# A sandwich layer on one core: new orders for the mixing stage's queues, one burst of scores per group, and gating moved to VectorE

## The chip, the cores and the metric

The kernel runs on one NeuronCore of a Trainium2 chip. The metric is the device time of one execution in microseconds. TensorE is written PE, VectorE DVE, ScalarE ACT, GpSimd POOL; SP is the engine that only issues transfers.

## The reference

All data is float32. x is (8, 512, 256): 8 batch rows of 512 time steps.

```python
x = x + layernorm(attn(layernorm(x)))
x = x + layernorm(ffn(layernorm(x)))
# attn: gate, value_raw, params = x @ W_in.T;  value = silu(causal_conv4(value_raw))
# dt = clip(softplus(params0 + dt_bias));  kd = 0.5 * sigmoid(params1);  A = exp(A_log)
# bc = l2norm over 32 states of (value @ W_bc.T): Bz, Bx, Cz, Cx, for each of 32 heads
def step(carry, inp):          # 512 steps, state (32 heads, 32 states, 16 channels)
    S = 1.0 / (1.0 + dt * kd + dt * dt * A)
    z = S * (z - dt * A * s + dt * Bz * u)
    s = s + dt * z + dt * Bx * u
    y = sum_n(Cz * z) + sum_n(Cx * s)
# out = ((y + skip * value) * silu(gate)) @ W_out.T
# ffn: gelu(x @ ternary(W1).T + b1) @ ternary(W2).T + b2
```

## The kernel before, in words

`build` calls three stages, one after the other, each with its own block of five instruction queues: `project` (L83), `mix` (L423) and `ffn` (L1246). They hand their results over in DRAM scratch tensors. A `Signal` (L51) is a semaphore whose target for row b and item i is computed by `at`. It is credited: negative items are taken as already given.

**project** normalises x, multiplies by W_in, convolves, and writes value, gate, skip x value x gate, u and the step factors. The change leaves it alone.

**mix** turns the recurrence into chunks of 64 steps (8 chunks in a row). The 32 heads form 8 groups of 4 heads (4 x 32 states = 128 partitions); a batch row is done in two halves of 4 groups, here called phases: 16 phases in all, and `over_rows` loops over the batch rows, the last one written apart. In a phase, for its groups first to first + 3 and for the groups of the next half, `then` to then + 3:
- PE makes the next half's B and C by units (`product`, L689; 4 units per group, 4 matmuls of 128x512 over the contraction index kt per unit, into two PSUM banks used in turn), 5 units more than a half ahead. After a group's first unit it makes the previous group's sums of squares (`sum_squares`, L685). Between units it transposes keys (`transposes`, L714), multiplies them with u (`state_terms`, L726), makes the masked scores' products (`scores_and_unit`, L744: two pairs of heads, each 32 matmuls of 32x64, recorded as 64, each pair followed by half a unit), and the outputs (`outputs`, L766: 64 small matmuls with `g` and 28 with the block states `Xb`).
- ACT squares and copies each unit out of PSUM, starts the next load of weights, takes the root of the sums (`norms`, L822), copies transposed keys to `kT` (L857), states to `X` and `Xb`, and results to `y`.
- SP takes the norms of a group through a compact layout (`compact_norms`, L561), stores the finished scales to DRAM and loads them back spread over partitions, first the two for B (`input_scales`, L590), then, into the same buffer, the two for C (`output_scales`, L599). Every step is a wait followed by issues, in the order in L611 to L634. `load_valT` (L574) refills the moving operand of all units once per row, after unit 31 is done.
- POOL issues the loads of `shear` and `det`.
- DVE does, in the order written out in `phase` (L1194 to L1237): `scales` (L1024, on 128x64: waits for `compact`, counts `rows_ready`), `scale_inputs` (L1037, waits for SP's load, counts `b_scaled`), `scale_outputs` (L1045, the same, `c_scaled`), `keys` (L1069), `queries` (L1087), `det_sums`, `coefficients` (L1130), `states` (L1147, a chain over 7 chunks) and `mask` (L1120: ps_g x causal into `g`, once the outputs of the previous group have read it). Between all of these, `advance` interleaves the next phase's 128 psi steps (L1016, L1020) in proportion to a cost in ns that each operation gives; `advance(OF_PHASE)` issues those that are left.

`scores_and_unit` waits for `q_ready(group)` and for `g_ready(group - 1)`, as the score banks are single. `outputs` waits for `g_ready(group)`.

**ffn** works row by row. POOL gates y (`y * gate + svg`, L1387 and L1389, 128x2048 each). PE projects (`project_out`), ACT copies, DVE adds the normalised result to x (`first_residual`), normalises again (`second_norm`), PE transposes. The first product is taken in 8 tiles f with x split into a high and a low part (L1436), ACT applies Gelu (L1494) and copies the high part (L1496), DVE subtracts for the low part (L1598), PE makes the second product in four tiles t (L1449, 64 matmuls), DVE adds the bias (L1609), takes statistics of all four tiles, ACT takes the root (L1508), DVE normalises `o2` in place (L1531), adds x1 (L1621), ACT stores. Rows 0, 1, 6 and 7 are written out; 2 to 5 are a hardware loop of two rows. At the start SP loads y, gates, then both weights, which DVE makes ternary with three passes each (L1579 to L1582).

The order of PE's work in the second part of a phase, which the change touches:

```python
scores_and_unit(b, first, unit, last)
products(b, unit + 1, 1, last)
unit += 2
for i in range(1, HALF):
    scores_and_unit(b, first + i, unit, last)
    outputs(b, first + i - 1)
    products(b, unit + 1, 1, last)
    unit += 2
outputs(b, first + HALF - 1)
```

## Time and profile before

| what | us |
|---|---|
| median of 3 runs (2637.96 to 2643.87) | 2638.85 |
| the profiled execution | 2637.77 |
| its span | 2636.1 |
| PE busy | 2092.6 (79%) |
| DVE busy | 1921.2 (73%) |
| ACT busy | 956.8 (36%) |
| POOL busy | 385.6 (15%) |

The span runs from the first to the last instruction of one profiled execution; a busy time is the union of an engine's instructions. An engine's idle time before an instruction is put down to what released it last. PE's clock has two levels here, 1.0 (2.4 GHz) and 0.5 (1.2 GHz); a window's clock is the mean of what was granted. The stages are, by the span's time, `project` to about 294 us, `mix` to 2308 and `ffn` to the end.

### The profile page before, as it was taken

The page shows a single profiled execution, that of the slowest core. Times are in us where ns is not written, and L with a number is a line of the kernel's source. Part 1 is how long each engine was busy: PE and PEld are TensorE (multiplying, and loading weights), DVE is VectorE, ACT ScalarE, POOL GpSimd, SP SyncE. Part 2 cuts the span into 40 slices and gives each one's busy share as a digit, 9 for nine tenths or more (in the row PEclk, how much of TensorE's full clock was granted, in tenths as well). Part 3 has the DMA queues.
Part 4 walks back from the last instruction along what each step waited for, and adds up shares of the span by engine and source line. Part 5 has one row for each costly group of instructions (what it writes and reads, how often), then busy time and mean ns, then how long its engine had stood idle before and what let it go on. Part 6 is the DMA issues. An engine that isn't in the chain of part 4 may idle for free. (4 is left out here: it accounts for less than half of the span.)

```text
span 2636.1 us, 66597 instructions
## 1 busy us (share of the span) xinstructions
PE 2092.6 (79%) x25890; PEld 1258.7 (48%) x25890; DVE 1921.2 (73%) x4396; ACT 956.8 (36%) x1905; POOL 385.6 (15%) x604
## 2 busy tenths in 40 slices
PE   5777485887888988888878789998988887728886
PEld 2333132454454545444544445454544446626675
...
GB/s 96 172 171 163 148 127 82 134 100 131 96 137 99 131 103 136 109 111 131 104 129 97 135 95 130 115 135 111 107 134 101 137 83 85 14 253 127 127 25 24
DMA packets 240466, 306.05 MB, mean 116 GB/s; under 512 B 124960, under 2 KB 141344, under 8 KB 231968
## 3 DMA queue, kind: packets, MB, share of 16 engines
...
q10 hardware_dynamic: 85056, 94.40, 12.8%
...
## 5 line engine op out<-in xcount | busy, mean ns | idle before, releaser
L700 PE MATMUL m_ps_a<-m_valT,m_w_bc 128*128 128x512 f32 x2048 | 1037.3, 651 | 59.5 <-DMA m_valT<-scratch_valT 49.2
L700 PEld LDWEIGHTS m_ps_a<-m_valT,m_w_bc 128*128 128x128 f32 x2048 | 397.3, 206 | 472.9 <-issue 443.7
L651 POOL DMA_DIRECT2D m_shear<-scratch_shear x512 | 274.3, 537 | 1564.8 <-DVE m_psi L1020 1452.8
L835 ACT ACTIVATE m_sq<-m_ps_a 128x512 f32<-128x512 f32 x256 | 153.1, 598 | 651.7 <-PE m_ps_a L700 651.7
L759 PE MATMUL m_ps_g<-m_raw 32*64 32x64 f32 x8192 | 185.9, 249 | 166.9 <-DVE m_g L1124 141.3
L1020 DVE TENSOR_TENSOR m_psi<-m_psi,m_prod 128x128 f32<-128x128 f32 x1024 | 294.0, 287 | 19.6
L1016 DVE TENSOR_TENSOR m_prod<-m_psi,m_shear 128x128 f32<-128x128 f32 x1024 | 293.0, 286 | 18.0
L759 PEld LDWEIGHTS m_ps_g<-m_raw 32*64 32x64 f32 x8192 | 165.0, 159 | 268.4 <-issue 265.9
L1042 DVE TENSOR_TENSOR m_raw<-m_raw,m_scale 128x1024 f32<-128x1024 f32 x64 | 78.4, 1224 | 239.0 <-DMA m_scale<-scratch_norm 230.3
L784 PE MATMUL m_ps_k<-m_raw,m_Xb 128*112 128x64 f32 x1024 | 177.1, 306 | 0.0
L1079 DVE TENSOR_TENSOR m_part<-m_raw,m_psi 128x1024 f32<-128x1024 f32 x128 | 155.6, 1218 | 13.7 <-issue 13.2
L224 PE MATMUL ps_w<-p_xnT,w_in 128*128 128x512 f32 x256 | 130.5, 663 | 41.1 <-ACT vraw L282 36.0
L1110 DVE TENSOR_TENSOR m_part<-m_raw,m_psi 128x1024 f32<-128x1024 f32 x128 | 155.6, 1218 | 0.1
L784 PEld LDWEIGHTS m_ps_k<-m_raw,m_Xb 128*112 128x112 f32 x1024 | 150.9, 216 | 8.5 <-issue 3.7
L837 ACT ACTIVATE m_raw<-m_ps_a 128x512 f32<-128x512 f32 x256 | 152.5, 596 | 0.0
L897 ACT ACTIVATE m_y<-m_ps_y 112x256 f32<-112x256 f32 x64 | 24.6, 384 | 305.1 <-PE m_ps_k L784 305.1
L1124 DVE TENSOR_TENSOR m_g<-m_ps_g,m_causal 128x1024 f32<-128x1024 f32 x64 | 78.0, 1219 | 74.4 <-PE m_ps_k L784 74.3
L784 PE MATMUL m_ps_y<-m_raw,m_Xb 128*112 128x64 f32 x768 | 130.4, 303 | 0.0
L877 ACT ACTIVATE m_Xb<-m_X 32x224 f32<-32x224 f32 x256 | 98.7, 386 | 74.9 <-DVE m_X L1165 71.8
L1050 DVE TENSOR_TENSOR m_raw<-m_raw,m_scale 128x1024 f32<-128x1024 f32 x64 | 78.1, 1220 | 60.5 <-DMA m_scale<-scratch_norm 60.5
L784 PEld LDWEIGHTS m_ps_y<-m_raw,m_Xb 128*112 128x112 f32 x768 | 114.1, 218 | 0.0
L224 PEld LDWEIGHTS ps_w<-p_xnT,w_in 128*128 128x128 f32 x256 | 52.2, 212 | 115.8 <-issue 66.0
...
## 6 DMA issues: line engine op xcount, KB each, us to landing
m_scale<-scratch_norm SPq DMA_DIRECT2D x512, 128.0 KB
...
m_shear<-scratch_shear POOLq DMA_DIRECT2D x512, 64.0 KB, 2.9
...
```

The source lines that it names most:

```text
L224: mm = pe.matmul(ps_w[i % BANKS].ap(), w_in[:, k, col:col + P], xnT[:, k, :], start=(k == 0), stop=(k == KD - 1))
L651: pool.dma_start(shear[h * N:(h + 1) * N, w % 2].rearrange("p k g t -> p k (g t)"), spread(src)).then_inc(into.sem, into.step)
L700: mm = pe.matmul(ps_a[j % 2].ap(), w_bc[:, j, kt, :], valT[:, kt, :], start=(kt == 0), stop=(kt == KI - 1))
L759: mm = pe.matmul(ps_g[odd * C:(odd + 1) * C, at:at + C], raw[heads, group, p_, cols], raw[heads, group, NJ - 1 - p_, cols], start=(p_ == 0 ...
L784: mm = pe.matmul(ps_y[c % 2][0:ROWS, c // 2 * C:(c // 2 + 1) * C], Xb[:, c - 1, p_, :], raw[:, group, NJ - 1 - p_, c * C:(c + 1) * C], sta ...
L835: act.activation(sq[:, j, :], ps_a[j % 2].ap(), ACT.Square).then_inc(sq_ready.sem, sq_ready.step)
L837: act.activation(raw[:, group % HG, j, :], ps_a[j % 2].ap(), ACT.Copy).then_inc(raw_ready.sem, raw_ready.step)
L877: ins = act.activation(Xb[heads, :, :, h * N:h * N + DH], X[heads, 0:NC - 1, :, group % HALF, :], ACT.Copy)
L1016: dve.tensor_tensor(prod.ap().rearrange("p k g r -> p (k g) r"), psi_kt[of_half][:, :, t, :], window.unsqueeze(2).to_broadcast([P, 2 * HAL ...
L1020: ins = dve.tensor_tensor(psi_t[of_half][:, :, :, t + 1, :], psi_t[of_half][:, :, :, t, :], prod[:, ::-1, :, :], ALU.add)
L1079: dve.tensor_tensor(in_pairs(part[:, k]), pairs(raw[:, slot, k, :]), psi[:, half % 2, k, g_, :, at:at + C, :], ALU.mult).then_inc(own.sem, ...
L1110: dve.tensor_tensor(in_pairs(part[:, k]), pairs(raw[:, group, 3 - k, :]), psi[:, half, k, g_, :, 1:, :], ALU.mult).then_inc(own.sem, own.o ...
```

## The change

In `mix`: SP and DVE issue the steps of the scales in a new order; the masked scores go in turn to `g` and to `kT`, so that a mask waits for the outputs of two groups back; the first mask of a phase is issued in the middle of `states`; each quarter of valT is loaded when unit 31's matmul on it is done; `scores_and_unit` becomes `scores` (both pairs, 64 matmuls recorded as 128) followed by whole units. In `ffn`: gating moves from POOL to DVE, three rows ahead; the second product, its bias and statistics go in two halves with the transposes between them; PE's projection goes in two parts; the normalisation and residual of a row are issued at the start of the next; all rows are written out; both weights are loaded from ACT's queue, and are made ternary in two passes each.

```diff
@@ -477,6 +477,7 @@
+        masked = [g.ap(), kT.ap().rearrange("p a (b h c) -> p a b h c", b=2, h=HP)]
@@ -503,6 +504,7 @@
+        val_used = sig("val_used", KI - 1)
@@ -573,6 +575,8 @@
 
     def load_valT(b):
         for kt in range(KI):
+            if not (isinstance(b, int) and b == 0):
+                sp.wait_ge(val_used.sem, val_used.at(b - 1, kt)) if kt < KI - 1 else sp.wait_ge(a_made.sem, a_made.at(b - 1, UNITS - 1))
             sp.dma_start(valT[:, kt, :], dram["valT"][b, :, kt, :]).then_inc(val_in[kt].sem, val_in[kt].step)
 
     def load_e_end(b, half):
@@ -622,14 +626,12 @@
                 input_scales(b, then + 1)
                 output_scales(b, then + 1)
                 norm_rows(b, then + 2)
+                input_scales(b, then + 2)
             if half == 0 and not last:
-                sp.wait_ge(a_made.sem, a_made.at(b, UNITS - 1))
                 load_valT(b + 1)
             if more:
-                input_scales(b, then + 2)
                 output_scales(b, then + 2)
                 norm_rows(b, then + 3)
-            if more:
                 input_scales(b, then + 3)
                 output_scales(b, then + 3)
     over_rows(sp, body)
@@ -699,6 +701,8 @@
+            if unit == UNITS - 1 and kt < KI - 1:
+                mm.then_inc(val_used.sem, val_used.step)
@@ -741,7 +745,7 @@
-    def scores_and_unit(b, group, unit, last):
+    def scores(b, group):
@@ -761,7 +765,6 @@
-            product(b, unit, last, pair * 2, pair * 2 + 2)
@@ -776,7 +779,7 @@
-                              u[rows, s, tile, h * DH:(h + 1) * DH], g[rows, h % 2, h // 2, tile, :],
+                              u[rows, s, tile, h * DH:(h + 1) * DH], masked[s % 2][rows, h % 2, h // 2, tile, :],
@@ -798,11 +801,12 @@
                 products(b, unit + 1, 1, last)
                 state_terms(b, first + i)
                 unit += 2
-            scores_and_unit(b, first, unit, last)
-            products(b, unit + 1, 1, last)
+            scores(b, first)
+            products(b, unit, 2, last)
             unit += 2
             for i in range(1, HALF):
-                scores_and_unit(b, first + i, unit, last)
+                scores(b, first + i)
+                products(b, unit, 1, last)
                 outputs(b, first + i - 1)
                 products(b, unit + 1, 1, last)
                 unit += 2
@@ -1120,8 +1124,8 @@
-        dve.wait_ge(y_made.sem, y_made.at(b, group - 1))
-        dve.tensor_tensor(g.ap().rearrange("p a h c t -> p (a h c) t"),
+        dve.wait_ge(y_made.sem, y_made.at(b, group - 2))
+        dve.tensor_tensor(masked[group % 2].rearrange("p a h c t -> p (a h c) t"),
@@ -1144,7 +1148,7 @@
-    def states(b, half, advance):
+    def states(b, half, advance, between):
@@ -1165,6 +1169,8 @@
+            if c == NC // 2 - 1:
+                between()
@@ -1206,35 +1212,33 @@
         det_sums(b, half, advance)
         if more:
             scale_outputs(b, then, advance)
+            scales(b, then + 1, advance)
         keys(b, first + 3, advance)
         queries(b, first, advance)
+        if more:
+            scale_inputs(b, then + 1, advance)
         queries(b, first + 1, advance)
         if more:
-            scales(b, then + 1, advance)
+            scale_outputs(b, then + 1, advance)
+            scales(b, then + 2, advance)
         coefficients(b, half, advance)
-        states(b, half, advance)
-        mask(b, first, advance)
+        states(b, half, advance, lambda: mask(b, first, advance))
         if more:
-            scale_inputs(b, then + 1, advance)
+            scale_inputs(b, then + 2, advance)
         queries(b, first + 2, advance)
         mask(b, first + 1, advance)
         if more:
-            scale_outputs(b, then + 1, advance)
-            scales(b, then + 2, advance)
+            scale_outputs(b, then + 2, advance)
+            scales(b, then + 3, advance)
         queries(b, first + 3, advance)
-        if more:
-            scale_inputs(b, then + 2, advance)
         mask(b, first + 2, advance)
         if more:
-            scale_outputs(b, then + 2, advance)
-            scales(b, then + 3, advance)
+            scale_inputs(b, then + 3, advance)
         advance(OF_PHASE)
-        if more:
-            scale_inputs(b, then + 3, advance)
         mask(b, first + 3, advance)
         if more:
+            scale_outputs(b, then + 3, advance)
             keys(b, then, stepping(b, half + 2, not last))
-            scale_outputs(b, then + 3, advance)
 
     def body(b, last):
         for half in range(2):
@@ -1322,22 +1326,16 @@
-        o2_made = sig("o2_made", 1)
+        o2_made = sig("o2_made", 2)
@@ -1380,14 @@
-@block.gpsimd
-def _(pool):
-    pool.sem_inc(gated.sem, gated.given * gated.step)
...
-        pool.tensor_tensor(y[s].ap(), y[s].ap(), gate[s].ap(), ALU.mult).then_inc(own.sem, own.one())
-        pool.wait_ge(own.sem, own.n)
-        pool.tensor_tensor(y[s].ap(), y[s].ap(), svg[s].ap(), ALU.add).then_inc(gated.sem, gated.step)
...
-    rows(pool, body)
@@ +1418,32 @@
+    def second(b, half_):
+        for t in range(2 * half_, 2 * half_ + 2):
+            for f in range(KF):
+                for part in (gh, gl):
+                    mm = pe.matmul(ps_2[half_][:, t % 2, :], part[:, f, t * P:(t + 1) * P], t2[:, f, :],
...
+        mm.then_inc(o2_made.sem, o2_made.step)
+
+    def body(b, s, left):
+        pe.wait_ge(xl_ready.sem, xl_ready.at(b, KD - 1))
+        for f in range(2):
+            hidden(b, f)
+        if left > 1:
+            for t in range(2):
+                project_out(b + 2, s, t)
+        for f in range(2, KF):
+            hidden(b, f)
+        if left > 1:
+            for t in range(2, TT):
+                project_out(b + 2, s, t)
+        pe.wait_ge(gl_ready.sem, gl_ready.at(b, KF - 1))
+        pe.wait_ge(o2_ready.sem, o2_ready.at(b, -1))
+        second(b, 0)
+        if left:
+            transpose_xn(b + 1)
+        second(b, 1)
@@ +1449,2 @@
+    for n, (dst, name) in enumerate(((w1, "w1T"), (w2, "w2T"))):
+        act.dma_start(dst.ap(), a[name].rearrange("(k p) o -> p k o", p=P)).then_inc(weight_in[n], 16)
@@ -1536,7 +1530,14 @@
-    def first_residual(b, s, i):
+    def gating(b):
+        s = b % 2
+        dve.wait_ge(y_in[s].sem, y_in[s].at(b // 2, y_in[s].per - 1))
+        dve.tensor_tensor(y[s].ap(), y[s].ap(), gate[s].ap(), ALU.mult).then_inc(own.sem, own.one())
+        dve.wait_ge(own.sem, own.n)
+        dve.tensor_tensor(y[s].ap(), y[s].ap(), svg[s].ap(), ALU.add).then_inc(gated.sem, gated.step)
+
+    def first_residual(b, s):
@@ +1566,30 @@
+    def second_bias(b, half_):
+        dve.wait_ge(o2_made.sem, o2_made.at(b, half_))
+        rows_ = range(2 * half_, 2 * half_ + 2)
+        ins = dve.tensor_tensor(o2[:, 2 * half_:2 * half_ + 2, :], ps_2[half_].ap(),
+                                b2.ap().unsqueeze(1).to_broadcast([P, 2, D]), ALU.add)
+        if half_:
+            ins.then_inc(o2_ready.sem, o2_ready.step)
+            dve.wait_ge(o2_ready.sem, o2_ready.at(b, 0))
+        else:
+            ins.then_inc(own.sem, own.one())
+            dve.wait_ge(own.sem, own.n)
+        for t in rows_:
+            dve.bn_stats(stats2[:, t, :], o2[:, t, :]).then_inc(own.sem, own.one())
+        dve.wait_ge(own.sem, own.n)
+        for t in rows_:
+            ins = dve.bn_aggr(mv[2][:, t, :], stats2[:, t, :])
+            ins.then_inc(own.sem, own.one()) if t < TT - 1 else ins.then_inc(var2_ready.sem, var2_ready.step)
+    def second_residual(b):
+        dve.wait_ge(sd2_ready.sem, sd2_ready.at(b, 0))
+        dve.reciprocal(rstd[2].ap(), sd[2].ap()).then_inc(own.sem, own.one())
+        dve.wait_ge(own.sem, own.n)
+        normalise(on, lambda t: o2[:, t, :], 2)
+        dve.wait_ge(own.sem, own.n)
+        dve.wait_ge(res_stored.sem, res_stored.at(b, -1))
+        dve.tensor_tensor(res.ap(), x1[b % 2].ap(), on.ap(), ALU.add).then_inc(res_ready.sem, res_ready.step)
+        dve.wait_ge(res_ready.sem, res_ready.at(b, 0))
@@ -1579,20 @@
-        dve.tensor_scalar(above.ap(), w, half[:, n:n + 1], None, ALU.is_gt).then_inc(own.sem, own.one())
-        dve.tensor_tensor(tern.ap().rearrange("p k o -> p (k o)"), above.ap(), below.ap(),
-                          ALU.subtract).then_inc(ternary_ready, 1)
+        dve.scalar_tensor_tensor(out=tern.ap().rearrange("p k o -> p (k o)"), in0=w, scalar=half[:, n:n + 1],
+                                 in1=below.ap(), op0=ALU.is_gt, op1=ALU.subtract).then_inc(ternary_ready, 1)
+        if n == 0:
+            gating(1)
@@ +1627,25 @@
+    def body(b, s, left):
+        if b:
+            second_residual(b - 1)
         for f in range(KF):
             dve.wait_ge(gh_ready.sem, gh_ready.at(b, f))
             dve.tensor_tensor(gl[:, f, :], g[:, f, :], gh[:, f, :].bitcast(F32), ALU.subtract).then_inc(gl_ready.sem, gl_ready.step)
             if left and f == KF // 2 - 1:
-                first_residual(b + 1, 1 - s, i + s)
+                first_residual(b + 1, 1 - s)
         if left:
             second_norm(b + 1, 1 - s)
         if left > 1:
             projection_moments(b + 2)
+        second_bias(b, 0)
         if left:
             low_part(b + 1)
-        dve.wait_ge(o2_made.sem, o2_made.at(b, 0))
-        for half_ in range(2):
-            ins = dve.tensor_tensor(o2[:, 2 * half_:2 * half_ + 2, :], ps_2[half_].ap(),
-                                    b2.ap().unsqueeze(1).to_broadcast([P, 2, D]), ALU.add)
-            ins.then_inc(o2_ready.sem, o2_ready.step) if half_ else ins.then_inc(own.sem, own.one())
-        moments(lambda t: o2[:, t, :], 2, var2_ready)
...
-        normalise(o2, lambda t: o2[:, t, :], 2)
...
+        if left > 2:
+            gating(b + 3)
+        second_bias(b, 1)
...
```

## Rows read from the trace of the kernel before

**Rows 1.** Windows: stretch, length, PE PEld DVE ACT POOL busy (count), clock, DMA.
```profile
473.80:2159.60 1685.80, 1454.40 (x21282) 838.67 (x21281) 1326.41 (x3095) 611.86 (x1302) 267.15 (x502) 0.89 0.44 117
2159.60:2308.00 148.40, 103.94 (x2137) 89.81 (x2135) 95.00 (x181) 35.40 (x86) 8.32 (x16) 0.56 0.20 53
2308.00:2374.00 66.00, 19.11 (x75) 15.64 (x75) 38.39 (x50) 5.32 (x10) 27.01 (x6) 0.66 0.79 254
2374.00:2636.10 262.10, 202.68 (x1016) 171.04 (x1016) 176.16 (x387) 120.43 (x191) 45.90 (x10) 0.86 0.22 75
```

**Rows 2.** L1135, first instruction of `coefficients`: count, ns min/median/max, first and last start.
```profile
L1135 DVE TENSOR_TENSOR m_end<-m_det,m_e_end x16: 190/194/197, 473.8 to 2251.3; 128x28 f32<-128x28 f32 x16
```

**Rows 3.** Groups by line, DVE: busy us, mean ns | idle before, releasers.
```profile
L1042 DVE TENSOR_TENSOR m_raw<-m_raw,m_scale 128x1024 f32<-128x1024 f32 x64 | 78.4, 1224 | 239.0 <-DMA m_scale<-scratch_norm 230.3 <-ACT m_raw L837 6.9 <-issue 1.8
...
L1050 DVE TENSOR_TENSOR m_raw<-m_raw,m_scale 128x1024 f32<-128x1024 f32 x64 | 78.1, 1220 | 60.5 <-DMA m_scale<-scratch_norm 60.5
...
L1124 DVE TENSOR_TENSOR m_g<-m_ps_g,m_causal 128x1024 f32<-128x1024 f32 x64 | 78.0, 1219 | 74.4 <-PE m_ps_k L784 74.3
...
L1027 DVE TENSOR_SCALAR m_compact<-m_compact 128x64 f32<-128x64 f32 x64 | 12.1, 189 | 37.3 <-DMA m_compact<-m_rows 37.3
```

**Rows 4.** Groups by line, PE, same columns.
```profile
L759 PE MATMUL m_ps_g<-m_raw 32*64 32x64 f32 x8192 | 185.9, 249 | 166.9 <-DVE m_g L1124 141.3 <-issue 24.3 <-DVE m_raw L1116 0.3
...
L778 PE MATMUL m_ps_y<-m_g,m_u 64*16 64x64 f32 x2048 | 47.8, 241 | 68.8 <-DVE m_g L1124 68.8
...
L700 PE MATMUL m_ps_a<-m_valT,m_w_bc 128*128 128x512 f32 x2048 | 1037.3, 651 | 59.5 <-DMA m_valT<-scratch_valT 49.2 <-issue 7.4 <-ACT m_raw L837 2.8
```

**Rows 5.** Timeline of DVE in one phase: start us, us, line [idle before].
```profile
1760.73 0.23 DVE L1034 TENSOR_TENSOR m_compact<-m_compact,m_factor 128x64 f32<-128x64 f32 x1
...
1768.87 1.23 DVE L1042 TENSOR_TENSOR m_raw<-m_raw,m_scale 128x1024 f32<-128x1024 f32 x1 [2.55 <-DMA m_scale<-scratch_norm]
...
1830.36 0.22 DVE L1034 TENSOR_TENSOR m_compact<-m_compact,m_factor 128x64 f32<-128x64 f32 x1
...
1843.38 1.23 DVE L1042 TENSOR_TENSOR m_raw<-m_raw,m_scale 128x1024 f32<-128x1024 f32 x1 [5.01 <-DMA m_scale<-scratch_norm]
...
1849.87 1.22 DVE L1050 TENSOR_TENSOR m_raw<-m_raw,m_scale 128x1024 f32<-128x1024 f32 x1 [2.75 <-DMA m_scale<-scratch_norm]
...
1853.06 0.20 DVE L1027 TENSOR_SCALAR m_compact<-m_compact 128x64 f32<-128x64 f32 x1 [1.43 <-DMA m_compact<-m_rows]
```

**Rows 6.** The same timeline: `queries(first)` and `queries(first + 1)` begin.
```profile
1785.74 1.22 DVE L1093 TENSOR_TENSOR m_raw<-m_raw,m_det 128x1024 f32<-128x1024 f32 x1
...
1793.32 1.22 DVE L1093 TENSOR_TENSOR m_raw<-m_raw,m_det 128x1024 f32<-128x1024 f32 x1
```

**Rows 7.** Timeline of PE: start us, us, line; same phase, then the last phase.
```profile
1812.90 1.98 PE L759 MATMUL m_ps_g<-m_raw 32*64 32x64 f32 x64 [6.97 <-DVE m_g L1124]
...
1829.13 1.07 PE L685 MATMUL m_ps_s<-m_sq,m_head_sum 128*32 128x512 f32 x8
...
2260.84 4.04 PE L759 MATMUL m_ps_g<-m_raw 32*64 32x64 f32 x128 [6.10 <-DVE m_g L1124]
```

**Rows 8.** Windows of that phase's second half and of the last phase, columns of rows 1.
```profile
1812.90:1819.30 6.40, 6.40 (x96) 3.75 (x100) 5.94 (x14) 0.34 (x1) 2.14 (x4) 0.50 0.51 128
...
2187.90:2308.00 120.10, 85.28 (x1843) 78.47 (x1835) 72.55 (x115) 27.78 (x69) 3.82 (x8) 0.50 0.19 50
```

**Rows 9.** Groups by line, feed-forward stage, columns of rows 3; last: of rows 2.
```profile
L1531 DVE TENSOR_SCALAR f_o<-f_o,f_mv,f_rstd 128x256 f32<-128x256 f32 x32 | 33.7, 1115 | 0.3
...
L1609 DVE TENSOR_TENSOR f_o<-f_ps,f_b 128x512 f32<-128x512 f32 x16 | 10.3, 686 | 52.3 <-PE f_ps L1449 52.3
...
L1389 POOL TENSOR_TENSOR f_y<-f_y,f_svg 128x2048 f32<-128x2048 f32 x8 | 36.7, 4590 | 0.6
...
L1531 DVE TENSOR_SCALAR f_o<-f_o,f_mv,f_rstd x32: 400/408/4735, 2410.2 to 2631.0; 128x256 f32<-128x256 f32 x32
```

**Rows 10.** L1621, last DVE instruction of a row: columns of rows 2.
```profile
L1621 DVE TENSOR_TENSOR f_res<-f_x,f_o x8: 1224/1224/1227, 2416.7 to 2631.5; 128x1024 f32<-128x1024 f32 x8
```

108 lines of the change are left out of this document (38 added, 70 removed).

## The prediction

> **What bounds the kernel now.** The profiled execution took 2637.77 us (span 2636.1 and 1.7 around it), 1.1 below the median of the three runs, 2638.85; all sums below start from 2637.8. I read the page first (PE 79% busy, DVE 73%: no engine is full), then windows by stage, the idle time by line, and the timeline of single phases. The mixing stage is 1.7 ms of 2.6: 14 equal phases fill 1685.8 us, 120.4 each, with DVE busy 94.7 and PE 103.9 in each [rows 1, 2]. At the mean clock of 0.89 some 26 us of a phase run at 1.2 GHz, so PE's work at 2.4 GHz would be about 104 - 13 = 91 us. Neither engine can be the bound alone at 120: they wait for each other and for DMA, in a ring.
>
> The waits are these. DVE stands for the normalising scales, which go by SP out to DRAM and back, 230.3 and 60.5 us; before the mask, 74.3, until the outputs of the previous group have left `g`; for `compact`, 37.3 [rows 3]. PE stands for the masked scores, 141.3 and 68.8 us [rows 4]. One trip of the scales takes from `rows_ready` to the scaled input 7.9 us in the one case and 12.8 in the other [rows 5]. The input of `then + 2` and `then + 3` have little DVE work in that time, so DVE waits; PE, behind it, waits too, falls to 1.2 GHz and works more slowly when it resumes, as at 1812.90 after 6.97 us of idleness [rows 7, 8].
>
> **The change, mixing stage.** (1) DVE's order: each `scales` is issued one place earlier, so that more vector work covers a trip. A 128x1024 operation with its share of psi steps costs 1.9 us (`queries`, 7.6 us [rows 6], is four such by size). After the change the cover is: input `then`, one `keys`, 5.7, unchanged; `then + 1`, `keys` and `queries`, 13.3; `then + 2`, coefficients, states and one mask, about 11.5; `then + 3`, `queries` and a mask, 9.5. Against trips of 7.9 to 12.8 [rows 5] that leaves waits of 3.0, 0.5, 0.5 and 1.0. Output scales follow `b_scaled` by 5.3 us or so (input begins 1843.38 and lasts 1.2, output begins 1849.87 [rows 5]): all have 7.6 or more of cover, except `then + 3`, which now stands ahead of `keys(then)` and has a mask and the last five steps, 2.7 us. I put 3.8 there, a new wait (bounds 0 and 6).
>
> (2) `scales(then + 3)` now stands before `queries(first + 3)`. It needs the sum of squares that PE makes after unit 32. From the first scores after `mask(first)` to the end of that sum PE took 1812.90 to 1830.20, 17.3 us [rows 7], and the burst changes the order within it, not the work. The square root, four issues on SP and the landing I estimate at 4.9 (the whole tail of input scale, output issues and compact took 8.5, 1844.6 to 1853.06 [rows 5], and is the upper bound). DVE has in that time three of seven state steps (3.8 by the code's own costs), input scale, `queries`, mask and output scale, together 17.1. So 5 us of waiting stand there that did not before (bounds 0 and 9).
>
> (3) The second masked buffer lets `mask(g)` wait for `y_made(g - 2)`: the 74.3 us go [rows 3], a part of them in the last phase. That `g_made` is not the next wait rests on the `queries` between; were PE a whole `outputs` late, 1 to 2 us a mask would stay. `mask(first)` in mid-states lets PE resume 4 us earlier, and is the start of the chain in (2). PE's two mask waits per group become one long one, about 9 us at the second group, since PE needs 91 of the period.
>
> (4) The burst: a group's two score halves follow each other, then a whole unit. The last phase has the same form already: 128 recorded matmuls took 4.04 us at half clock, against 1.98 for 64 [rows 7]; no price, within 0.1 us a group. If PE's queue can't fetch so many small ones at 2.4 GHz, up to 1 us a group, in PE's slack.
>
> (5) valT by quarters, loads released by `val_used`: part of 49.2 us of PE waits [rows 4]; the one at the stage's start stays. On SP it is now behind `input_scales(then + 2)` but ahead of the output scales, which wait with it for unit 31 in every first half: 3 to 4 us late, inside the 9.5 of cover. Priced 0, bounds -5 and +10 us in all.
>
> DVE is idle 25.7 us in each of the 14 phases [rows 1]. The four waits are 402.4 us, 25.2 for each of 16 phases [rows 3]; a part of that lies before the first phase and in the last, and some 2 us of the 25.7 are gaps between instructions, so I take 23.5 for a middle phase. After: 5.0 for input scales, 3.8, 5.0, and nothing for masks: 13.8, less 0.3 where one delay hides another. That is 10 us a phase, a period near 110.5. The sum: 14 x 10 = 140, 8 in the interval after, and 6 in the last phase.
>
> By the Trainium skill ("DMA: Bandwidth & Descriptors", Latency and other measured facts) a transfer has a fixed cost of about 2 us, so two hops would be some 4 and the input waits would vanish. Rows 5 say 7.9 and more; with the page's figure the period would be about 105.
>
> **The change, feed-forward stage.** A row takes (2631.5 - 2416.7) / 7 = 30.7 us, and over the whole stretch 262.1 / 8 = 32.8 [rows 1, 10]. Removed: GpSimd's two products (4.59 and about the same again [rows 9]), and with them the stall of DVE's normalisation of `o`, 1115 ns mean where the median is 408 [rows 9], (1115 - 408) x 4 = 2.8 us a row, and by an estimate half as much, 1.5, at the other two normalisations. Added: the same two on DVE, four 128x1024 pieces at 1.22 [rows 3], 4.9 us a row. DVE waits 52.3 / 8 = 6.5 a row for the second product [rows 9]; gating now lies in that gap, and the product is split so that its bias and statistics start half way and only half of them (1.6 us) precede the next row's Gelu; the normalisation and residual of the row move into the next row's Gelu time, 3 us. Sum: 4.9 - 4.3 added, 1.6 + 3 taken from the chain, and about 1 for the projection in two parts: 5 a row, 40 in all over 8 rows. One pass fewer on the weights and their load on ACT's queue move the start by 0 to 5 us; the first row still waits for the same bytes at 254 GB/s [rows 1]. Priced 0. Bounds of the stage: -3 (gating fully exposed) and 60 (all of DVE's 6.5 too).
>
> The forecast: 2637.8 - 140 - 8 - 6 - 40 = 2444, say 2445 us.
>
> **Rivals.** A, waits change place: the new chain of (2) costs its 9, the output wait 6, feed-forward gives 25. For it: SP is one queue, and each trip is issued behind a wait. Phase gain 5: 2637.8 - 70 - 8 - 6 - 25 = 2529. B, trips shorten once less collides, and nearly no DVE wait remains: period 105, which is DVE's 94.7 busy [rows 1], 2 of gaps and 8 for the two trips without cover, 2637.8 - 14 x 15.4 - 14 - 45 = 2363. Against: DMA gets denser with a shorter period. C, slower: PE stays at 1.2 GHz. The one long idle stretch ahead of a burst of 32-row matmuls is where the clock falls; the last phase, all burst and outputs, ran at 0.50 for 120 us while PE was 71% busy [rows 8]. With x us of a phase's full-clock work at half clock the period is 91 + x and a few us; beyond x = 32, 123.3, the loss exceeds the feed-forward's gain. With x = 40, period 133: 2637.8 + 176 - 40 = 2774. Against: in 1812.90 to 1819.30 the clock came back after 6.4 us with the same bursts between units [rows 8], and 512-wide units follow here as there.
>
> By the Trainium skill ("TensorE: Matmul & The Clock Gate", Part 4) transposes do not count as PE activity, which speaks for C in each phase's first half; rows 1's 0.89 for the same mixture does not bear it out. D: the order helps but gating on DVE makes that engine the feed-forward's bound, gain 0 there: 2484. That burst and order change nothing at all is excluded by the instructions moved.
>
> **Chances and range.** Forecast and its neighbourhood (2395 to 2490, D within it) 0.62, A 0.18, B 0.13, C 0.04, and 0.03 for gains and losses that cancel. The range goes from 2380 to 2535, leaving out C, the farther half of B and the edge of A. A measurement of this kernel tells about 0.2%, 5 us. Faster 0.94, same 0.01, slower 0.05.
>
> **What would show it.** L1135's starts 110 us apart (right), 116 or more (A), 106 or less (B). L1042's wait for scales under 6 us a phase, L1124's gone, L1027's near 5, L1050's near 4. One PE wait a phase of 8 to 10 us at L759; granted clock over the phases 0.89 or above; below 0.8 is C. Feed-forward rows 28 us apart, no wait at the bias above 3. Wrong would be: a DVE wait that none of these names, or PE idle for less than 3 us a phase.

## The result and the profile after

The changed kernel took 2480.61 us (median of 4 runs, 2478.51 to 2491.96) beside 2638.55 for the kernel before on the same chip: a ratio of 0.9406 [0.9375, 0.9437], 158 us less. The forecast was 2445 and the range 2380 to 2535: faster as said, inside the range and 35.6 us above the likeliest value. The profiled execution took 2482.11 us, its span 2480.4. On another chip the same kernel gave 2482.13, ratio 0.9414 [0.9389, 0.9439]. The kernel before has medians of 2630.6 to 2638.9 on the chips used, so what is compared below is ratios.

The windows by stage, in the columns and for the stages of [rows 1]. The bounds moved with the stages: the first to the fifteenth start of `coefficients`, then to the end of `mix`, then the feed-forward's start, then its rows.

```profile
482.40:2062.30 1579.90, 1426.94 (x21285) 823.59 (x21283) 1322.34 (x3095) 612.50 (x1303) 267.26 (x504) 0.91 0.46 125
2062.30:2190.10 127.80, 97.72 (x2128) 86.77 (x2128) 90.00 (x170) 34.25 (x84) 6.20 (x12) 0.57 0.19 51
2190.10:2235.00 44.90, 9.36 (x34) 7.70 (x34) 15.90 (x13) 2.37 (x3) 0.00 (x0) 0.61 0.94 262
2235.00:2480.40 245.40, 200.28 (x1056) 160.07 (x1056) 193.99 (x439) 121.30 (x198) 0.00 (x0) 0.95 0.28 101
```

The 14 middle phases take 1579.9 us where they took 1685.8: 112.85 each, against 120.4 before and 110.5 forecast. DVE is busy 94.5 us in each, as before; what went is its idle time. The first line of `coefficients` [rows 2] and the feed-forward's residual [rows 10], by source line, give the rest:

```profile
L1139 DVE TENSOR_TENSOR m_end<-m_det,m_e_end x16: 193/196/200, 482.4 to 2138.9; 128x28 f32<-128x28 f32 x16
```
```profile
L1591 DVE TENSOR_TENSOR f_res<-f_x,f_on x8: 1224/1225/1226, 2289.6 to 2475.9; 128x1024 f32<-128x1024 f32 x8
```

`mix` ends (the feed-forward's first DVE instruction) at 2190.1 where it ended at 2309.3: 119.2 us less, where 154 were forecast. That is 105.9 in the 14 phases, 15.0 in the interval after (91.6 to 76.6), 6.8 in the tail, less 8.6 by which the first start came later. The feed-forward stage takes 290.3 us instead of 326.8: 36.5 less, where 40 were forecast. Its rows end 27.8 us apart at first and 26.6 in the mean, against 30.7 before and 28 forecast. Nearly the whole miss is in the mixing stage's phases.

The groups by line over the whole execution, DVE's and PE's, answer to [rows 3, 4]:

```profile
L1046 DVE TENSOR_TENSOR m_raw<-m_raw,m_scale 128x1024 f32<-128x1024 f32 x64 | 78.2, 1223 | 111.9 <-DMA m_scale<-scratch_norm 111.9
L1054 DVE TENSOR_TENSOR m_raw<-m_raw,m_scale 128x1024 f32<-128x1024 f32 x64 | 78.2, 1221 | 65.8 <-DMA m_scale<-scratch_norm 65.8
...
L1128 DVE TENSOR_TENSOR m_g<-m_ps_g,m_causal 128x1024 f32<-128x1024 f32 x32 | 39.0, 1219 | 1.0 <-PE m_ps_g L763 1.0
L1128 DVE TENSOR_TENSOR m_kT<-m_ps_g,m_causal 128x1024 f32<-128x1024 f32 x32 | 39.0, 1218 | 9.6 <-PE m_ps_g L763 9.6
...
L1031 DVE TENSOR_SCALAR m_compact<-m_compact 128x64 f32<-128x64 f32 x64 | 12.2, 191 | 93.0 <-DMA m_compact<-m_rows 93.0
```
```profile
L702 PE MATMUL m_ps_a<-m_valT,m_w_bc 128*128 128x512 f32 x2048 | 1029.1, 651 | 68.5 <-DMA m_valT<-scratch_valT 45.4 <-issue 17.4 <-ACT m_raw L841 5.7
...
L763 PE MATMUL m_ps_g<-m_raw 32*64 32x64 f32 x8192 | 200.3, 261 | 140.5 <-DVE m_g L1128 110.6 <-issue 22.7 <-DVE m_raw L1120 1.8
```

The input scales' wait has halved, the masks' has fallen from 74.4 to 10.6 (all of it behind the middle phases), `compact`'s has grown by 56, the output scales' by 5. PE's second mask wait (68.8 at the outputs) is gone. This is the pattern the forecast drew. Its sizes need the same view cut to the 14 middle phases, which the prediction didn't take. Before (473.8 to 2159.6):

```profile
L1042 DVE TENSOR_TENSOR m_raw<-m_raw,m_scale 128x1024 f32<-128x1024 f32 x56 | 68.6, 1224 | 206.4 <-DMA m_scale<-scratch_norm 197.7 <-ACT m_raw L837 6.9 <-issue 1.8
L1050 DVE TENSOR_TENSOR m_raw<-m_raw,m_scale 128x1024 f32<-128x1024 f32 x56 | 68.3, 1219 | 41.6 <-DMA m_scale<-scratch_norm 41.6
L1124 DVE TENSOR_TENSOR m_g<-m_ps_g,m_causal 128x1024 f32<-128x1024 f32 x56 | 68.2, 1219 | 45.7 <-PE m_ps_k L784 45.6
...
L1027 DVE TENSOR_SCALAR m_compact<-m_compact 128x64 f32<-128x64 f32 x56 | 10.6, 189 | 13.2 <-DMA m_compact<-m_rows 13.2
```

and after (482.4 to 2062.3):

```profile
L1083 DVE TENSOR_TENSOR m_part<-m_raw,m_psi 128x1024 f32<-128x1024 f32 x112 | 136.7, 1220 | 21.7 <-issue 21.3 <-DVE m_prod L1020 0.4
...
L1046 DVE TENSOR_TENSOR m_raw<-m_raw,m_scale 128x1024 f32<-128x1024 f32 x56 | 68.5, 1222 | 82.7 <-DMA m_scale<-scratch_norm 82.7
L1054 DVE TENSOR_TENSOR m_raw<-m_raw,m_scale 128x1024 f32<-128x1024 f32 x56 | 68.4, 1221 | 45.6 <-DMA m_scale<-scratch_norm 45.6
...
L1031 DVE TENSOR_SCALAR m_compact<-m_compact 128x64 f32<-128x64 f32 x56 | 10.7, 191 | 69.5 <-DMA m_compact<-m_rows 69.5
```

A middle phase had (206.4 + 41.6 + 45.7 + 13.2) / 14 = 21.9 us of named waits, not 23.5, and has (82.7 + 45.6 + 69.5) / 14 = 14.1, not 13.5. (Of the 206.4 the scales' DMA ended 197.7; with that part alone the 21.9 would be 21.3.) The 21.7 before L1083 is a gap inside `keys` of about 3 us once a row, where the loop over the rows turns: 1.5 a phase, 0.9 before (13.2 over 14 phases). By place, the timeline has the input scales waiting 3.2 us at `then`, nothing at `then + 1` and `then + 2`, and 2.7 at `then + 3`.

### The profile page after: what moved, and what is told of

Its sections match the earlier page's. It is cut to its first block and busy times, and to the rows that moved or that the text cites. A ratio compares the mean times of both kernels' runs of the same rounds, so it can differ in the third digit from the quotient of the medians.

```text
span 2480.4 us, 66343 instructions
## 1 busy us (share of the span) xinstructions
PE 2055.9 (83%) x25890; PEld 1226.2 (49%) x25890; DVE 1912.4 (77%) x4410; ACT 955.2 (39%) x1905; POOL 311.4 (13%) x588
## 5 line engine op out<-in xcount | busy, mean ns | idle before, releaser
L702 PEld LDWEIGHTS m_ps_a<-m_valT,m_w_bc 128*128 128x128 f32 x2048 | 407.8, 209 | 524.4 <-issue 502.8
L763 PE MATMUL m_ps_g<-m_raw 32*64 32x64 f32 x8192 | 200.3, 261 | 140.5 <-DVE m_g L1128 110.6
L1020 DVE TENSOR_TENSOR m_prod<-m_psi,m_shear 128x128 f32<-128x128 f32 x1024 | 292.4, 286 | 15.7
L763 PEld LDWEIGHTS m_ps_g<-m_raw 32*64 32x64 f32 x8192 | 178.0, 170 | 189.1 <-issue 172.5
L1083 DVE TENSOR_TENSOR m_part<-m_raw,m_psi 128x1024 f32<-128x1024 f32 x128 | 155.8, 1220 | 22.3 <-issue 21.3
L787 PE MATMUL m_ps_k<-m_raw,m_Xb 128*112 128x64 f32 x1024 | 156.4, 279 | 0.1
L787 PEld LDWEIGHTS m_ps_k<-m_raw,m_Xb 128*112 128x112 f32 x1024 | 131.1, 191 | 7.4 <-issue 0.8
L787 PE MATMUL m_ps_y<-m_raw,m_Xb 128*112 128x64 f32 x768 | 115.0, 276 | 0.0
L1387 PE MATMUL f_ps_o<-f_w_out,f_y 128*128 128x256 f32 x256 | 63.9, 407 | 48.0 <-DVE f_y L1538 48.0
L742 PEld LDWEIGHTS m_ps_k<-m_u,m_kT 64*32 64x32 f32 x7168 | 69.1, 109 | 62.6 <-issue 62.4
L787 PEld LDWEIGHTS m_ps_y<-m_raw,m_Xb 128*112 128x112 f32 x768 | 98.7, 191 | 0.0
```

The source lines that it names most:

```text
L702: mm = pe.matmul(ps_a[j % 2].ap(), w_bc[:, j, kt, :], valT[:, kt, :], start=(kt == 0), stop=(kt == KI - 1))
L763: mm = pe.matmul(ps_g[odd * C:(odd + 1) * C, at:at + C], raw[heads, group, p_, cols], raw[heads, group, NJ - 1 - p_, cols], start=(p_ == 0 ...
L787: mm = pe.matmul(ps_y[c % 2][0:ROWS, c // 2 * C:(c // 2 + 1) * C], Xb[:, c - 1, p_, :], raw[:, group, NJ - 1 - p_, c * C:(c + 1) * C], sta ...
L1020: dve.tensor_tensor(prod.ap().rearrange("p k g r -> p (k g) r"), psi_kt[of_half][:, :, t, :], window.unsqueeze(2).to_broadcast([P, 2 * HAL ...
L1083: dve.tensor_tensor(in_pairs(part[:, k]), pairs(raw[:, slot, k, :]), psi[:, half % 2, k, g_, :, at:at + C, :], ALU.mult).then_inc(own.sem, ...
```

## The chain inside one phase

The timeline of PE, DVE and SP's queue in one phase shows step (2) of the forecast at work (lines between left out):

```profile
1502.73 4.04 PE L763 MATMUL m_ps_g<-m_raw 32*64 32x64 f32 x128 [5.02 <-DVE m_g L1128]
...
1519.32 1.06 PE L687 MATMUL m_ps_s<-m_sq,m_head_sum 128*32 128x512 f32 x8
1520.31 2.41 PE L763 MATMUL m_ps_g<-m_raw 32*64 32x64 f32 x128
```
```profile
1501.37 1.22 DVE L1128 TENSOR_TENSOR m_g<-m_ps_g,m_causal 128x1024 f32<-128x1024 f32 x1
...
1525.27 0.20 DVE L1031 TENSOR_SCALAR m_compact<-m_compact 128x64 f32<-128x64 f32 x1 [5.22 <-DMA m_compact<-m_rows]
...
1541.25 1.22 DVE L1046 TENSOR_TENSOR m_raw<-m_raw,m_scale 128x1024 f32<-128x1024 f32 x1 [5.29 <-DMA m_scale<-scratch_norm]
```
```profile
1521.15 2.74 SPq L567 DMA_DIRECT2D m_compact<-m_rows  x4
1526.41 0.35 SPq L597 DMA_DIRECT2D scratch_norm<-m_compact  x1
1532.40 11.81 SPq L574 DMA_DIRECT2D m_scale<-scratch_norm  x8
```

The first mask releases PE, whose burst begins at 1502.73; the sum of squares ends at 1520.38, 17.65 us later (forecast 17.3); `compact` is there at 1525.27, 4.9 later (forecast 4.9); DVE has waited 5.22 (forecast 5). Then the trip to DRAM: the store is issued at 1526.41, and the loads wait for it until 1532.40, 6 us for the first hop alone. The scaled input starts at 1541.25, 14.8 us after the store was issued. The trips were taken as 7.9 to 12.8 [rows 5].

This phase is the second half of a row. In the seven second halves DVE waits 5.2 us in the mean for `compact` of `then + 3`. In the seven first halves it waits 2.6 there, since it has stood 3.7 for the output scales of `then + 2` just before. The rest of `compact`'s 69.5 us lies at other groups, 1.1 a phase.

## Experiments

Every kernel below computes the whole result. Ratios are against the kernel before on the same chip; a "period" is the distance of the first and fifteenth start of `coefficients`, divided by 14, in the profiled execution. It comes from that one execution: the changed kernel has 112.85, and 112.70 on the other chip.

**The two stages apart.** `mix_only` has `mix` as changed and `ffn` as before, `ffn_only` the reverse. Each is the diff above up to this line of `ffn`, or from it on:

```diff
-        o2_made = sig("o2_made", 1)
+        o2_made = sig("o2_made", 2)
```

> The new mixing stage with the feed-forward stage of before. In the two traces the mixing stage ends 119.2 us earlier and the feed-forward stage is 36.5 us shorter. If the two stages are independent: 2638.6 - 119 = 2519 us, and the phases stay 112.8 us apart. If a part of the gain of one stage comes from the other (caches of instructions, state left by the stage ahead), the sum of this run's gain and the next one's differs from 158 by more than 5 us.

> The mixing stage of before with the new feed-forward stage. Independent stages: 2638.6 - 37 = 2602 us.

Measured: 0.9542 [0.9495, 0.9588], period 112.59, and 0.9848 [0.9799, 0.9896], feed-forward stage 292.4 us. The two gains add to 0.0610, the whole change's is 0.0594. The difference is well inside the intervals, which would hide an effect of one stage on the other up to some 18 us; the period and the stage's length in the two traces, 0.3 and 2.1 us from the changed kernel's, show none. Three quarters of the gain is the mixing stage's.

**One masked buffer again.**

```diff
-        masked = [g.ap(), kT.ap().rearrange("p a (b h c) -> p a b h c", b=2, h=HP)]
+        masked = [g.ap(), g.ap()]
...
-                    dve.wait_ge(y_made.sem, y_made.at(b, group - 2))
+                    dve.wait_ge(y_made.sem, y_made.at(b, group - 1))
```

> After, but all masked scores go to g, so that a mask waits for the outputs of the group before, as in before. The forecast gave the second buffer the 74.3 us of mask waits. If it is worth that now: the mask of groups 1 to 3 waits for y_made 3 to 5 us a phase, 50 to 75 us slower, 2530 to 2555. If the order of DVE alone had removed them (more vector work between two masks): 0 to 15 us slower.

Measured: 0.9562 [0.9523, 0.9601], period 115.36. The mask's wait in the 14 middle phases is back, and part of the others has gone:

```profile
L1046 DVE TENSOR_TENSOR m_raw<-m_raw,m_scale 128x1024 f32<-128x1024 f32 x56 | 68.4, 1221 | 82.9 <-DMA m_scale<-scratch_norm 82.9
L1128 DVE TENSOR_TENSOR m_g<-m_ps_g,m_causal 128x1024 f32<-128x1024 f32 x56 | 68.3, 1219 | 66.3 <-PE m_ps_k L787 65.9
...
L1054 DVE TENSOR_TENSOR m_raw<-m_raw,m_scale 128x1024 f32<-128x1024 f32 x56 | 68.2, 1218 | 27.6 <-DMA m_scale<-scratch_norm 27.5
...
L1031 DVE TENSOR_SCALAR m_compact<-m_compact 128x64 f32<-128x64 f32 x56 | 10.6, 189 | 56.5 <-DMA m_compact<-m_rows 56.5
```

A wait of 66 us costs 2.5 x 14 = 35 in the phases: the other half is taken from the output scales (45.6 to 27.6) and from `compact` (69.5 to 56.5), which had been waiting while DVE now stands elsewhere. By its ratio the kernel is some 40 us slower than the changed one, between the two expectations: the order of DVE had not removed the wait, but the buffer is worth less than its wait.

**The first mask behind `states` again.**

```diff
-                    states(b, half, advance, lambda: mask(b, first, advance))
+                    states(b, half, advance, lambda: None)
+                    mask(b, first, advance)
```

> After, with the first mask behind the states again. By the chain that I gave (mask, scores, unit 31, outputs, unit 32, sum of squares, compact) everything from there on comes 3.8 us later while DVE's work up to scales(then + 3) is the same in sum, so the wait at compact grows by 3.8 us a phase, less what the outputs had waited for Xb: 30 to 55 us slower, 2511 to 2536. Rival (the chain is bound at Xb, which the states make, not at the mask): within 10 us of after.

Measured: 0.9654 [0.9616, 0.9692], period 117.3, 4.45 more than the changed kernel; by its ratio some 65 us slower, more than either theory had said. `compact` waits 100.6 us in the 14 phases (7.2 a phase for 5.0) and the scales 159.6 (11.4 for 9.2); PE's clock over them is 0.90, and PE's own wait for a mask at the scores 150.8 us for 97.8. Of the pieces of the mixing stage that were taken back it is the largest. PE is released later by the states' second half, and the chain to the last scales starts that much later. In second halves this falls on `compact` of `then + 3` (9.1 us for 5.2), in first halves on the output scales of `then + 2` (7.3 for 3.7), which stand behind unit 31.

**The scores' two pairs apart again**, each ahead of half a unit, all else as changed.

```diff
-                def scores(b, group):
+                def scores_and_unit(b, group, unit, last):
...
+                        product(b, unit, last, pair * 2, pair * 2 + 2)
```

> After, with the score pairs apart again and half a unit behind each, all else as after. My theory (the burst has no price, what misses from the 140 us was a size of the waits): 2481 within 5 us. Rival (the burst holds PE up by 2 us or more a phase, in fetch or clock, and that is a part of the 34 us that the phases fell short): faster by 14 us or more, under 2467. A gain from the burst itself: over 2486.

Measured: 0.9370 [0.9334, 0.9406], period 111.58, clock over the phases 0.93 against 0.91. PE's group of the scores in the middle phases, after and with the pairs apart:

```profile
L763 PE MATMUL m_ps_g<-m_raw 32*64 32x64 f32 x7168 | 170.2, 256 | 124.2 <-DVE m_g L1128 97.8 <-issue 20.1 <-DVE m_raw L1120 1.8
```
```profile
L763 PE MATMUL m_ps_g<-m_raw 32*64 32x64 f32 x7168 | 152.7, 239 | 130.4 <-DVE m_g L1128 109.4 <-issue 16.6 <-DVE m_raw L1120 4.1
```

The burst makes the scores dearer by (170.2 - 152.7) / 14 = 1.25 us a phase, and PE more busy by 1.7, at a slightly lower clock. Step (4) gave it no price. The intervals of the two kernels overlap, so over the whole kernel it may cost nothing, and the ratio's equivalent of 2472 us lies between this run's two theories (2481 within 5, under 2467). A gain from the burst, which would have been a ratio above the changed kernel's, isn't seen: this part of the change is not where its time comes from.

**Three edits against the waits that are left**, each by itself. `valt_later` puts valT's loads behind the output scales of `then + 2`; `outputs_after_keys` puts the output scales of `then + 3` behind `keys(then)` again; `sums_early` makes the second unit, and so the sums of squares, ahead of the first group's outputs (ACT's `norms` moves with it).

```diff
+                            output_scales(b, then + 2)
                         if half == 0 and not last:
                             load_valT(b + 1)
                         if more:
-                            output_scales(b, then + 2)
```
```diff
-                        scale_outputs(b, then + 3, advance)
                         keys(b, then, stepping(b, half + 2, not last))
+                        scale_outputs(b, then + 3, advance)
```
```diff
                             scores(b, first + i)
-                            products(b, unit, 1, last)
+                            products(b, unit, 2 if i == 1 else 1, last)
                             outputs(b, first + i - 1)
-                            products(b, unit + 1, 1, last)
+                            if i > 1:
+                                products(b, unit + 1, 1, last)
```

> After, with SP's load_valT behind output_scales(then + 2) in place of ahead of it. In every first half of a row DVE waits 3.7 us for these scales; I had priced that at 0. If the wait comes from SP standing in load_valT for unit 31, it goes from 3.7 to under 0.5, 7 times; but the sum of squares behind it (compact, 2.3 to 5 us) is next, and takes most of it: 0 to 15 us faster, 2466 to 2481. If valT now lands later than unit 32 wants it: PE's wait for valT grows from 1.1 us and the run is no faster. If the wait is the DMA queues' own and not SP's order, 3.7 stays.

> After, with scale_outputs(then + 3) behind keys(then), as before. It loses the wait of 1.2 to 2.5 us that I had forecast as new at 3.8. But the next compact is then released no earlier, since SP issues it after the output load, which waits for nothing of DVE but b_scaled. 1.5 us a phase if nothing takes it: 20 us faster, 2461. If the wait passes on to the next trip (scale_inputs(then), which waits 3 to 4 us after scales): within 5 us of after.

> After, with unit 32 and the sum of squares behind it ahead of outputs(first), and ACT's root of it ahead of its copy of y. The sum comes 3.7 us earlier. If the new wait at compact is bound by this chain, it goes from 4.2 us a phase to under 1 and the period from 112.8 to 109.5: 2481 - 45 = 2436. Rival (another trip takes its place: the scales of then + 3, or in first halves the output scales behind load_valT, or valT itself, which unit 32 now wants 3.7 us sooner): under 20 us faster.

Measured: 0.9391 [0.9354, 0.9427], 0.9372 [0.9334, 0.9410] and 0.9360 [0.9313, 0.9406]; periods 111.88, 112.08 and 111.91. Waits a phase, from the groups of the middle phases: scales 9.2 after, then 6.5, 6.6 and 9.0; `compact` 5.0, then 6.6, 7.3 and 3.8. The first two edits remove their wait, and each time the next one grows: the scales' 2.6 us less of `valt_later` give 0.97 of period (in first halves the wait for `compact` of `then + 3` goes from 2.6 to 6.0), the 2.5 of `outputs_after_keys` give 0.77. `sums_early` is another case: `compact` loses 1.2 and the scales hardly change. In second halves it does what it should: the chain from the first burst to the sum takes 14.3 us instead of 17.6 in the mean, and the wait for `compact` of `then + 3` falls from 5.2 to 1.9. In first halves the chain takes 17.9 for 18.8 and that wait is 3.3 for 2.6, since unit 32, wanted sooner, now waits for valT, the rival that the expectation named. PE's group of the units in the middle phases, after and in `sums_early`:

```profile
L702 PE MATMUL m_ps_a<-m_valT,m_w_bc 128*128 128x512 f32 x1797 | 905.1, 651 | 24.9 <-issue 17.4 <-DMA m_valT<-scratch_valT 7.4
```
```profile
L702 PE MATMUL m_ps_a<-m_valT,m_w_bc 128*128 128x512 f32 x1796 | 887.4, 640 | 38.8 <-DMA m_valT<-scratch_valT 20.8 <-issue 17.8
```

All three intervals overlap the changed kernel's; that each by itself is faster is likely, not shown. From the first two I took it that the waits are one ring: each engine waits for the next all the way round, so that little more can be had by moving one wait.

**All three together**, without and with the pairs apart, and the changed kernel itself on the same chip.

> The changed kernel itself, unaltered, as the reference for the three kernels beside it on the same chip. Every theory expects the ratio of the first comparison again, 0.940 within 0.003; the differences of the others are to be read against this run and not against that of another chip.

> The three edits to the mixing stage's order that each gave 0.4 to 0.5 per cent or less, together: valT's loads behind the output scales of then + 2, the output scales of then + 3 behind keys(then), and the second unit and its sums of squares ahead of the outputs of the first group. If the waits are separate, the gains add: period 112.85 - 0.95 - 0.75 - 0.95 = about 110.2, 2640 x ratio 0.924. If they are a ring in which a wait taken away turns up at the next trip (my theory since the single runs), the period stays within 111 to 112, ratio 0.933 to 0.938, and the sum of DVE's waits changes by less than 1.5 us a phase while their places change.

> The same three, and the scores' two pairs each followed by half a unit again, as in the kernel before. The split alone gave a granted clock of 0.93 over the phases against 0.91 and a period of 111.6 against 112.85. If PE's clock is what the ring runs at, this is the fastest, period 110 to 111, ratio 0.928 to 0.934; if the split's gain was the same microsecond that the other edits take, it is within 2 us of the kernel beside it.

Measured: 0.9414 [0.9389, 0.9439], 0.9324 [0.9294, 0.9353] and 0.9320 [0.9289, 0.9351]. The DVE groups of `combined` in its 14 middle phases (there L1050 is the input scales' line, L1058 the output scales', L1035 `compact`'s):

```profile
L1050 DVE TENSOR_TENSOR m_raw<-m_raw,m_scale 128x1024 f32<-128x1024 f32 x56 | 68.4, 1221 | 80.7 <-DMA m_scale<-scratch_norm 80.7
...
L1058 DVE TENSOR_TENSOR m_raw<-m_raw,m_scale 128x1024 f32<-128x1024 f32 x56 | 68.2, 1218 | 0.0
...
L1035 DVE TENSOR_SCALAR m_compact<-m_compact 128x64 f32<-128x64 f32 x56 | 10.7, 192 | 92.1 <-DMA m_compact<-m_rows 92.1
```

The period of this execution is 110.23, what the single ones add to (112.85 - 0.97 - 0.77 - 0.94 = 110.17), and DVE's waits are 1.8 us a phase less than the changed kernel's, a little more than the 1.5 that a closed ring allowed. But the profile caught the quickest of five runs, 2440.86 us; the median is 14.5 longer, which over 14 phases would be a period near 111.3. `combined_split`, profiled 3 us above its median, has a period of 111.50, hardly less than the 111.58 of the pairs apart by themselves. The ratio lies between the ring's 0.933 to 0.938 and the 0.9295 to which the single gains add (0.9414 less 0.0023, 0.0042 and 0.0054), and its interval takes in both. So neither theory is shown wrong. What is shown is that the three together gain 0.9 per cent over the changed kernel on the same chip, with the intervals apart. Whether they gain more than `sums_early` by itself (0.9360 [0.9313, 0.9406]) isn't: those intervals overlap. At 2455.35 us beside 2482.13 this is the lowest median measured. With the pairs apart the ratio is the same: what they gave by themselves isn't seen on top of these.

**Gating back on GpSimd**, the rest of the feed-forward stage as changed.

```diff
-                def gating(b):
...
+            @block.gpsimd
+            def _(pool):
...
+                    pool.tensor_tensor(y[s].ap(), y[s].ap(), gate[s].ap(), ALU.mult).then_inc(own.sem, own.one())
+                    pool.wait_ge(own.sem, own.n)
+                    pool.tensor_tensor(y[s].ap(), y[s].ap(), svg[s].ap(), ALU.add).then_inc(gated.sem, gated.step)
```

> The feed-forward stage with gating back on GpSimd and all else as changed. By the forecast's terms gating costs DVE 4.9 us a row and gives back 4.3 of stalled normalisations, so with gating on GpSimd the stage should come out within about 5 us of the changed kernel's 290.3, with the normalisation of o back at a mean near 1.1 us where GpSimd's products overlap it. Rival 1: gating on DVE fills time in which DVE waited anyway, and the stalls behind GpSimd's shared port were on the chain; then this stage is 15 to 34 us longer, ratio 0.946 to 0.953. Rival 2: gating on DVE is on the chain and the new order alone brought the gain; then the stage is 10 to 35 us shorter, ratio 0.928 to 0.937.

Measured: 0.9558 [0.9531, 0.9584], feed-forward stage 326.8 us, to the tenth that of the kernel before. That is rival 1, and a little more than it said. So in the changed stage all 36.5 us hang on where gating runs, and the new order with gating on GpSimd brings nothing. That doesn't make the order worthless by itself: with gating on GpSimd DVE is busy 224.8 us in this stage where the kernel before had 214.4, so that the collisions described below cost more in the new order. The groups of the two normalisations, with gating on GpSimd and on DVE (over the stage; a 128x256 has a median of 408 ns in both):

```profile
L1536 DVE TENSOR_SCALAR f_on<-f_o,f_mv,f_rstd 128x256 f32<-128x256 f32 x32 | 42.2, 1379 | 0.3
L1536 DVE TENSOR_SCALAR f_on<-f_proj,f_mv,f_rstd 128x256 f32<-128x256 f32 x32 | 17.0, 593 | 0.3
...
L1573 DVE TENSOR_TENSOR f_o<-f_ps,f_b 128x512 f32<-128x512 f32 x16 | 11.1, 692 | 40.7 <-PE f_ps L1433 40.7
```
```profile
L1538 DVE TENSOR_TENSOR f_y<-f_y,f_svg 128x2048 f32<-128x2048 f32 x8 | 18.3, 2292 | 0.3
L1536 DVE TENSOR_TENSOR f_y<-f_y,f_gate 128x2048 f32<-128x2048 f32 x8 | 18.3, 2284 | 10.9 <-DMA f_svg<-scratch_svgT 10.9
...
L1525 DVE TENSOR_SCALAR f_on<-f_o,f_mv,f_rstd 128x256 f32<-128x256 f32 x32 | 11.1, 409 | 0.3
L1569 DVE TENSOR_TENSOR f_o<-f_ps,f_b 128x512 f32<-128x512 f32 x16 | 11.0, 690 | 20.7 <-PE f_ps L1422 20.7
```

One such meeting in the timeline, DVE then GpSimd:

```profile
2401.78 8.00 DVE L1536 TENSOR_SCALAR f_on<-f_o,f_mv,f_rstd 128x256 f32<-128x256 f32 x4
2409.82 1.23 DVE L1595 TENSOR_TENSOR f_res<-f_x,f_on 128x1024 f32<-128x1024 f32 x1
```
```profile
2399.75 4.55 POOL L1382 TENSOR_TENSOR f_y<-f_y,f_gate 128x2048 f32<-128x2048 f32 x1 [23.43 <-DMA f_y<-scratch_yT]
2404.37 4.61 POOL L1384 TENSOR_TENSOR f_y<-f_y,f_svg 128x2048 f32<-128x2048 f32 x1
```

Four normalisations that take 1.4 us take 8.0: they get on only as GpSimd's two products end, at 2404.30 and 2408.98. The two normalisations' stalls, (1379 - 409) x 32 ns = 31.0 us and 5.9, come to what gating costs DVE, 36.6. But they aren't all: DVE has 5 us more at the subtraction for the low part (L1630, mean 780 ns for 687) and 8 at the making of the ternary weights (L1611 and L1613, 3.5 and 4.4 us each for 1.3 and 2.4). Over the stage DVE is busy 224.8 us with gating on GpSimd and 209.9 with gating on DVE, 14.9 less (windows of the whole stage, below: before, gating on GpSimd, gating on DVE). The other 21.6 of the 36.5 us is idle time of DVE that went: its wait for the second product is 40.7 us there and 20.7 with gating in it. That the stalls counted so much because PE waits for the statistics behind them fits this, but is argued.

```profile
2309.30:2636.10 326.80, 221.79 (x1090) 186.68 (x1090) 214.44 (x437) 125.75 (x201) 72.91 (x16) 0.82 0.33 112
```
```profile
2190.40:2517.20 326.80, 217.61 (x1090) 183.39 (x1090) 224.75 (x435) 124.07 (x201) 74.34 (x16) 0.81 0.34 112
```
```profile
2190.10:2480.40 290.30, 209.64 (x1090) 167.77 (x1090) 209.89 (x451) 123.67 (x201) 0.00 (x0) 0.89 0.39 126
```

Between the first and the last residual the windows show what else it does (columns of [rows 1]), gating on GpSimd and on DVE:

```profile
2310.50:2512.70 202.20, 156.17 (x830) 133.43 (x828) 152.22 (x334) 93.75 (x152) 27.49 (x6) 0.86 0.22 76
```
```profile
2289.60:2475.90 186.30, 156.95 (x857) 125.17 (x856) 148.46 (x343) 101.49 (x165) 0.00 (x0) 0.98 0.23 82
```

PE is busy for the same time in a stretch that is 15.9 us shorter, and its granted clock is 0.98 for 0.86. These seven rows hold 15.9 of the 36.5 us; the other 20.6 lie ahead of the first residual. There DVE's busy time falls from 71.3 to 60.2 us, and the stalls are those of the ternary weights, of the first row's normalisation (7.3 us for 1.4) and of the subtractions behind it.

By the Trainium skill ("SBUF — State Buffer", Who interferes with whom) VectorE and GpSimd share a pair of ports; a VectorE instruction in its two-port mode contends for it, and whichever engine issues first holds the pair for its whole instruction while the other "fully blocks". The trace agrees with the blocking: 8.00 us where 1.38 is usual, ending with GpSimd's products. In which mode the normalisations ran it doesn't show.

## Why the prediction was right, and where it was short

The direction and the mechanism of the mixing stage were right, with one term of the sum too large; the feed-forward stage came out near its 40 us for another reason than the one given.

- *DVE's order, step (1).* Right in kind. Input scales wait 82.7 / 14 = 5.9 us a phase where 5.0 was said: 3.2, 0, 0 and 2.7 at the four groups for 3.0, 0.5, 0.5 and 1.0. A trip at the last group took 14.8 us where at most 12.8 was taken. Output scales wait 3.3 where 3.8 was said. That wait stands elsewhere: 1.4 at `then + 3`, and 3.7 at `then + 2` in every first half, behind valT's loads. That is step (5)'s "3 to 4 us late, inside the 9.5 of cover", priced 0: late by that much, and not inside. `valt_later` took 2.6 a phase out of the scales' waits and 0.97 out of the period.
- *The chain, step (2).* Right term by term in second halves: 17.65 and 4.9 in the phase shown, and a wait of 5.2 for the 5 that was said. `mask_late` shows that the chain starts at the first mask. In first halves the wait is 2.6, because the output scales' wait before it has taken the rest, and 1.1 a phase stands at other groups. That the sum is 4.96 a phase, as forecast, is in part luck. `sums_early` bears the chain out where valT is there in time, and shows that in first halves valT is next.
- *The second buffer, step (3).* The wait is gone, as said. PE's one long wait is 97.8 / 14 = 7.0, where about 9 was said. But `one_buffer` puts its worth at 2.5 us of period, where the middle phases had 45.7 / 14 = 3.3 us of this wait to lose and 4.7 come back.
- *The burst, step (4).* The scores take 1.25 us a phase more in it, 0.3 a group, where no price and at most 0.1 a group were said, or up to 1 if PE's queue were the limit. It also lies on the chain of (2), with 4.04 us at the first group. Rival C, a clock that stays down, didn't come: 0.91 for 0.89.
- **The mis-sized term is the base of the sum**: "so I take 23.5 for a middle phase". It was 21.9, to be read from the groups cut to the middle phases. The waits were taken over all 16 phases, but 28.7 of the masks' 74.3 us and 24.1 of `compact`'s 37.3 lie outside the 14 middle ones. That is 1.6 of the 2.4 us a phase. The waits after are 0.6 over the forecast's 13.5, and the loop's edge costs 0.6 more. These are 2.8; the busy time (0.3 less) and the small gaps give 0.4 back. Times 14 that is 34 of the 37.1 us by which the profiled execution missed; 1.2 of the 37.1 is the rounding up from 2444 to 2445, the other way. The first start's 8.6 and the interval's 15 - 8 = 7 all but cancel (scales that stood behind `coefficients` now stand ahead of it), the tail gave 0.8 more, the feed-forward stage 3.5 less.
- *Feed-forward.* 36.5 for 40: near in size, for a reason only half right, which makes the size luck in part. Gating cost 36.6 / 8 = 4.6 a row (forecast 4.9), and the stalls that it ends were (1115 - 408) x 32 ns at `o` [rows 9] and, by the same view, 6.7 and 6.1 us at the other two: 4.4 a row (forecast 4.3). But the sum set these off against each other, "4.9 - 4.3 added", and booked the order with 1.6 + 3 + 1 as the gain. `pool_gating` shows otherwise: the move gains 36.5 with the new order in place, and the order without the move nothing. The sum also left out the stalls at the low part's subtraction (L1598, in the view of [rows 9] 779 ns where 687 is the mean after), which is 5.9 us over the stage.
- *Rivals.* D, gating as DVE's bound, is out by the stage's 36.5 us, though its 2484 is only 2 us from the 2482.11 measured: it kept 154 us of the mixing stage and nothing of the other, the trace has 119.2 and 36.5. A's own prices (waits of 5, 6 and 9 against 23.5) leave a phase gain of 3.5, not 5, and give about 2550 where 2529 was written; the measured gain is 7.6 a phase. B didn't come either: the period is 112.85, not 105.

Not tried: gating on DVE in the old order, which would say whether the new one has a part in the 36.5; the first order of the scales with all else as changed, so that the worth of DVE's order in step (1) is read from the waits alone; and a scale trip without DRAM.
